# Dummy matmuls of the first stage taken out of a patch-embedding, Nyström attention and mixture-of-experts kernel

## The reference

```python
h = einsum('bnk,kd->bnd', patches(x, length=16, stride=8), W) + b      # 64 x 45 x 128
y = layernorm(h); z = layernorm(y) * gamma + beta, padded in front from 45 to 64 rows
q, k, v = split(z @ w_qkv)                         # 8 heads of 16, q scaled by 1/4; 64 landmarks of one row each
attn = softmax(q @ k.T)                            # the same matrix serves as attn1, attn2, attn3
z0 = attn.T / (max row sum * max column sum)       # maxima over all batches and heads
six times: z = 0.25 z (13 I - az (15 I - az (7 I - az))), az = attn @ z
h = h + y + (attn @ (z @ (attn @ v)) + conv33(v)) @ w_out + b_out
h = h + mixture of 8 experts (128 -> 256 -> 128, relu), the best two weighted by softmax, of layernorm(h)
```

## Time and profile before

| | before |
|---|---|
| median of 3 runs | 722.22 us (720.36 to 723.89) |
| the profiled execution's own time | 717.63 us |
| its span, first to last instruction | 715.8 us |
| TensorE matmul busy in the span | 689.8 us (96%) |
| VectorE, ScalarE, GpSimd busy | 381.4, 239.9, 302.0 us |
| mean granted TensorE clock | 0.998 |

### The profile page before, as it was taken

One profiled execution on the slowest core, in us unless ns is written; L12 is line 12 of the kernel. 1 busy time (PEld: TensorE's weight loads), 2 busy tenths in 40 slices (PEclk: granted clock), 3 DMA queues, 4 the chain that ended last, 5 costly groups with the idle time before them and its releaser, 6 DMA issues.

```text
span 715.8 us, 38807 instructions
## 1 busy us (share of the span) xinstructions
PE 689.8 (96%) x17423; PEld 593.4 (83%) x17423; DVE 381.4 (53%) x994; ACT 239.9 (34%) x453; POOL 302.0 (42%) x397
## 2 busy tenths in 40 slices
PE   1899999998999999999999999999999999999996
PEld 1688888876788788989898888899898989888875
DVE  4555555553453653655466466445655664564532
ACT  1355555543231231332223233323223241332342
POOL 3776666632742642642452353425426432432000
PEclk9999999999999999999999999999999999999999
DMA  2400000000000000000000000000000000000000
GB/s 58 131 13 11 10 10 10 2 3 3 4 5 5 4 4 5 4 4 4 14 4 4 14 4 5 3 15 5 4 4 14 4 4 14 5 4 4 12 12 10
DMA packets 8886, 7.99 MB, mean 11 GB/s; under 512 B 1676, under 2 KB 8228, under 8 KB 8740
## 3 DMA queue, kind: packets, MB, share of 16 engines
q1 hardware_dynamic: 6916, 3.09, 1.7%
q0 software_dynamic: 672, 2.12, 1.0%
q10 hardware_dynamic: 1152, 0.53, 0.3%
HBM read 4.26 MB, written 1.48 MB: 8 GB/s over the span
## 4 chain that ended last, share of the span: by engine, by line
PE 94%; issue 1%; DVE 1%; ACT 1%; POOL 1%; ACTq 0%; DMA 0%; DVEq 0%; POOLq 0%
PE bank L880 88%; PE bank L925 4%; PE bank L904 1%; PE bank L891 1%; PE bank L1030 0%; DMA bout_sb<-in_L_attn_b_out 0%; PE bank L1081 0%; PE bank L1042 0%; ACT hT L587 0%; DVE mx L673 0%; POOL rstd L335 0%; ACT L461 0%; DVE E L676 0%; ACT XT L496 0%; DVE nm L645 0%
## 5 line engine op out<-in xcount | busy, mean ns | idle before, releaser
L426 POOL TENSOR_TENSOR T<-Q,W 128x506 f32<-128x506 f32 x144 | 172.5, 1226 | 287.9 <-DVE W L743 265.6
L587 ACT ACTIVATE hT<-bank,b_sb 128x360 f32<-128x360 f32 x128 | 71.8, 561 | 254.1 <-PE bank L880 251.2
L752 DVE SCALAR_TENSOR_TENSOR P<-T,bank 128x506 f32<-128x506 f32 x144 | 95.7, 665 | 111.1 <-PE bank L880 106.9
L880 PEld LDWEIGHTS bank<-W 46*46 46x46 f32 x6144 | 136.8, 120 | 19.0 <-issue 18.2
L880 PEld LDWEIGHTS bank<-P 46*46 46x46 f32 x6144 | 137.2, 120 | 16.4 <-issue 9.8
L880 PE MATMUL bank<-P 46*46 46x46 f32 x6144 | 143.2, 205 | 1.9 <-ACT P L553 1.9
L880 PE MATMUL bank<-W 46*46 46x46 f32 x6144 | 142.8, 205 | 0.0
L743 DVE SCALAR_TENSOR_TENSOR W<-bank,P 128x506 f32<-128x506 f32 x144 | 95.4, 667 | 77.0 <-PE bank L880 76.9
L565 ACT ACTIVATE Q<-P 128x506 f32<-128x506 f32 x144 | 82.3, 606 | 69.1 <-DVE P L752 62.6
L880 PE MATMUL bank<-w_sb,hT 128*128 128x128 f32 x768 | 100.8, 282 | 0.0
L880 PEld LDWEIGHTS bank<-w_sb,hT 128*128 128x128 f32 x768 | 91.1, 192 | 4.8
(11 more groups left out here) (121 smaller groups left out, 616.8 us busy)
## 6 DMA issues: line engine op xcount, KB each, us to landing
w_sb<-in_L_ffn_w POOLq DMA_DIRECT2D x2, 1024.0 KB, 7.5
pat<-in_x SPq DMA_DIRECT2D x24, 60.0 KB
out<-outb SPq DMA_DIRECT2D x24, 60.0 KB
wqkv_sb<-in_L_attn_w_qkv ACTq DMA_DIRECT2D x1, 192.0 KB, 2.7
band<-scratch SPq DMA_DIRECT2D x2, 66.1 KB
cn<-in_consts ACTq DMA_DIRECT2D x1, 72.0 KB, 1.9
tokw_sb<-in_L_tok_W ACTq DMA_DIRECT2D x1, 64.0 KB, 2.8
tokb_sb<-in_L_tok_b ACTq DMA_DIRECT2D x1, 64.0 KB, 3.7
```

The source lines that it names most:

```text
L426: pool.tensor_tensor(out=T[g], in0=Q[g], in1=W[g], op=ALU.subtract).then_inc(s_t[g], 1)
L587: act.activation(hT[e % 2][f][:, 0:BT], bank[4 + f][:, 0:BT], ACT.Relu, bias=b1_sb[:, 2 * e + f:2 * e + f + 1]).then_inc(s_hT, 1)
L752: dve.scalar_tensor_tensor(out=P[g], in0=T[g], scalar=T_OUT, in1=squared(g), op0=ALU.mult, op1=ALU.subtract).then_inc(s_p[g], 1)
L880: return pe.matmul(out, lhsT, rhs, start=start, stop=stop, skip_group_check=True)
```

## The change

The function `keep_warm`, its call in `body` and the constant `WARM_A` are taken out. The dummies after the first stage (`WARM_B`) and those in the second (`WARM_C`) stay.

```diff
-WARM_A, WARM_B, WARM_C = 1, 5, 1
+WARM_B, WARM_C = 5, 1
...
-            def keep_warm():
-                for _ in range(WARM_A):
-                    mm(bank[3][:, 0:3 * D], ident, wqkv_sb[:, :])
-
             pe.wait_ge(s_wa, 16 * N_WA)
...
                     if ahead and g == 3:
                         patches(blk + 2)
-                    if g != 2:
-                        keep_warm()
```

## The result

The changed kernel takes 735.06 us (median of 4 runs, 732.29 to 739.79) beside 721.29 us for the kernel before on the same chip: ratio 1.0191, 95% interval 1.0140 to 1.0241. Forecast were 712.5 us, 704 to 720. The profiled execution took 732.29 us, span 730.5. Here and in the experiments a median is over all executions, while ratio and interval leave out those more than 1.5% above the fastest of the same kernel.

The account below looks back on a forecast made before the run. TensorE's own work was taken to bound the first stage; gains of 0.7 us (block 0), 6.8 (blocks 1 to 6) and 2.2 (block 7) sum to 9.7, so 722.2 - 9.7 = 712.5 us, range 704 to 720.

Parts of the forecast that it names:

- The clock: Cost of a lower TensorE clock after the change, taken as zero.
- rows 5: Profile rows of the last block: from 152.13 us TensorE did only turns, scores and products, then idled 0.71 us.
- The second rival: Clock falls at the new wait, once a block: seven episodes of 2.7 us, net +9.2, 731.4 us; 12%.
- turn of step 2: Blocks 1 to 6: starts 7.55 us into the block; two dummies out give 0.40 us, 1.08 becomes a wait for X.
- the third rival: Clock falls once or twice in block 0: +2.7 or +5.4 us, so 715.2 to 717.9 us; 12%.
- Block 0's dummies: Those of steps 0 and 1 in the first block lie before waits for X and give nothing.
- the transition at zero: Between the stages, before the maximum over partitions: no gain lost, though GpSimd sat idle 5.61 us there.
- The rival of a GpSimd bound: X of the last step in blocks 1 to 6 comes 1.5 us late: gain 2.9 us, 719.3 us; 6%.
- a dummy out: First stage: each dummy holds TensorE for 0.74 us, so all 24 would be 17.8 us at most.
- step 3: Last step of blocks 1 to 6: its dummy gives its full 0.74 us, next block 8.55 us after the turn.
- block 7: Last block of the first stage: three dummies out give 2.2 us, lower end 1.9.

Follow-up runs that it names:

- experiment 12: The changed kernel with 7 instead of 5 dummies in the transition behind the first stage: 730.85 us, ratio 1.0121 to the kernel before.
- experiment 2: Against the kernel before: all first-stage dummies out, and GpSimd issues X of step 1 ahead of the root's power; 735.77 us, ratio 1.019.
- experiment 6: Against the kernel before: no wide first-stage dummies, 32 matmuls of 46 columns in step 1 of every block; 723.52 us, ratio 0.9988.

## Why the prediction was wrong

**The step that failed** is the one headed The clock: "I take zero, since the stretch in rows 5 is nearest." That stretch has idle time of 0.71 us between narrow matmuls. The change makes waits of 0.94 us with no dummy near, and 19 of 30 such waits cost the clock, where none of 11 of at most 0.65 us did. The nearest row was shorter than the wait that I had forecast myself at 1.08 us. Even 0.71 us isn't harmless each time: in the third profile of changed the clock fell at 168.32 us, in the second of the two idle times of 0.71 us at the end of the stage.

**The second rival was right** in its place (the new wait before turn of step 2) and its sign, at 12%. It took seven episodes of 2.7 us, 18.9 in all; four came, the number from which it decides, of 1.6 to 4.7 us, 3.2 in the mean, and block 0, which the third rival had singly, lost 4.3. That makes 17.0 us, and the first stage became 8.85 us longer where the rival had 9.2: so near a hit is in part luck, since count and price were off in opposite ways. Of the distance from its 731.4 us to the measured 735.1 the profile shows the 5.7 us of the second stage, which it did not have.

**Block 0's dummies** were priced at nothing, with the idle time behind them as cover. The cover was real, and yet the step was wrong: an idle time lengthened from 0.86 to 1.51 us cost the clock in two of three profiles (in the first it had not risen yet). Block 0 ended at 45.1 to 45.6 us in the three profiles of changed and at 41.9 to 43.0 in the four of before: 2.8 us in the mean, and 3.7 in the first pair, of which the profile of before was the quickest of its four.

**What came out as worked out**: turn of step 2 at 7.56 us into the block (7.55 forecast), behind X, after a wait of 0.94 us (1.08 forecast), with nm at 1.38 us (1.39); no other new wait of TensorE in blocks 1 to 6; the transition at zero (GpSimd's idle time before the maximum 5.70 us, 5.61 before). The rival of a GpSimd bound did not occur.

**A term off in size**: a dummy out gives 0.65 us (3.54 less 2.89), not 0.74, where the step before has none either. The turn behind products takes 1.13 us where it takes 1.03 behind a dummy: 155.74 to 158.63 is 2.89 us for such a step, and 2.80 was measured behind a dummy. From turn of step 2 to the next block it took 8.75 us, not 8.55, so step 3 gave 0.54 and not 0.74. A full-clock block took 16.31 and not 16.1 us, block 7 gave 1.83 and not 2.2, under the lower end of 1.9, and the gain at full clock was 8.2 and not 9.7.

**The rule against the change** in the Trainium skill ("TensorE: Matmul & The Clock Gate", section "A second HAM failure mode: psum-queue depth-cycling") has short idle times between groups of matmuls send the clock to and fro. This case's traces agree with it for waits of 0.94 us without dummies (19 of 30), and not for waits of 0.65 us or less (0 of 11); with dummies in three of four steps 2 of 12 waits of 0.66 and 1.09 us cost the clock in blocks 1 to 6. The page's example has no length of idle time, and it was for me to set one.

**What stays open.** In the means of the profiles (before 721.6 us of span, changed 733.4) 8.2 of 11.8 us lie in the first stage and 3.5 in the second, whose code is the same. Low stretches stand in the second stage of both kernels, in three of four profiles of before. Whether the change makes them more frequent is not shown: experiment 12 speaks for it, the spread of the profiles allows chance. Why waits of the same length sometimes cost the clock and sometimes don't, and what a dummy near a wait does for it, was not found.

## What to carry to other kernels

A dummy matmul in a kernel bound by TensorE is priced twice, by its own duration and by the idle time that it covers; before one is taken out, list the waits that appear in its place, and keep the dummies (here one of three a block) that stand where TensorE would wait. Dummies in front of an idle time are free and may still be doing work. Others can stand where the engine idles anyway, ahead of the first heavy matmuls and in transitions: with both the same kernel became 1% faster instead of 2% slower, though neither filling alone showed a gain.

## What was not expected of the hardware

- Being busy held the full clock but did not always bring it back. In experiment 2, block 7, turns, scores and products kept TensorE busy for 30.55 of 33 us and the clock stayed at its lower level (1.2 GHz instead of 2.4) up to the wide dummies of the transition. In block 0 of the first profile of changed, TensorE was busy for all of the 22 us from 19 to 41 us, and every operation ran at the low level: turns 2.02 us, scores 1.51, products 1.89 (the clock row shows full speed there, since its first record is the rise at 41.22). In the changed kernel, low stretches of the first stage ended in or right behind the projections, but for the one that began at 168.32. At full clock narrow work without a wait, and the projections, held it (experiment 6, 103 us).
- At the low level the narrow operations are not twice as long by the row, but nearly: products 1.89 us instead of 1.08, scores 1.51 instead of 0.89, turn 2.02 instead of 1.13, projections of queries and keys 2.82 instead of 1.50. Over whole blocks a low stretch cost a little under half its length (block 1: 3.15 us for one of 6.8).
- The kernel before isn't free of low stretches either; they lie in its first 34 us and its second stage, and its times follow them: executions with a mean clock of 0.998 took 717.4 to 719.5 us, those with 0.986 took 723.3 to 724.2.
